# Edge counts of a two-layer GNN: windows of 6 destinations instead of 9, and a third of the window fetches issued by ScalarE

## The reference

```python
def _sage_sum(h, src, dst, Ws, Wn, b):
    h_neigh = jax.ops.segment_sum(h[src], dst, num_segments=N_NODES)
    return h @ Ws + h_neigh @ Wn + b
h = jnp.maximum(_layernorm(x, axis=-1), 0.0)
h = _sage_sum(h, src, dst, Ws1, Wn1, b1)
h = _sage_sum(h, src, dst, Ws2, Wn2, b2)
return x + h
```

## Time and profile before

| | us |
|---|---|
| median of 3 runs (lowest to highest) | 632.31 (631.12 to 633.39) |
| the profiled execution, own time | 634.33 |
| its span | 632.5 |
| TensorE busy | 618.4 (98%) |
| VectorE busy | 359.3 (57%) |
| GpSimd busy | 259.8 (41%) |
| ScalarE busy | 162.2 (26%) |

### The profile page before, as it was taken

One profiled execution on the slowest core, in us unless ns is written; L12 is line 12 of the kernel. 1 busy time (PEld: TensorE's weight loads), 2 busy tenths in 40 slices (PEclk: granted clock), 3 DMA queues, 4 the chain that ended last, 5 costly groups with the idle time before them and its releaser, 6 DMA issues.

```text
span 632.5 us, 8980 instructions
## 1 busy us (share of the span) xinstructions
PE 618.4 (98%) x3274; PEld 538.7 (85%) x3274; DVE 359.3 (57%) x543; ACT 162.2 (26%) x269; POOL 259.8 (41%) x234
## 2 busy tenths in 40 slices
PE   6999999999999999999999999999999999999996
PEld 5778777776999999999999987888888888888885
DVE  5764899761357456483412293135384867667563
ACT  5444443232011111101203111321234221222320
POOL 5232495111197586687820168204032204735000
PEclk9999999999999999999999999999999999999999
DMA  8711432232278967869761766444422235414153
GB/s 297 228 46 38 116 91 56 39 103 74 86 277 310 323 222 275 308 209 326 269 233 49 254 222 240 155 145 166 149 68 84 81 119 168 165 62 139 32 220 124
DMA packets 77128, 103.92 MB, mean 164 GB/s; under 512 B 25826, under 2 KB 44268, under 8 KB 77079
## 3 DMA queue, kind: packets, MB, share of 16 engines
q1 hardware_dynamic: 54550, 86.74, 41.0%
q10 hardware_dynamic: 22528, 16.53, 8.4%
HBM read 65.15 MB, written 38.10 MB: 163 GB/s over the span
## 4 chain that ended last, share of the span: by engine, by line
PE 94%; DVE 1%; POOL 1%; ACT 1%; DMA 1%; issue 1%; SPq 0%; ACTq 0%; POOLq 0%; DVEq 0%
PE PS L1368 30%; PE PS L1333 17%; PE PS L1205 15%; PE PS L1341 14%; PE PS L1405 13%; PE PS L1197 3%; PE PS L1231 1%; DMA xin<-x_in 1%; POOL W L615 0%; POOL norm L623 0%; ACT hbuf L777 0%; DVE HT L964 0%; ACT HT L768 0%; DVE stats L955 0%; DVE stats L956 0%
## 5 line engine op out<-in xcount | busy, mean ns | idle before, releaser
L1368 PE MATMUL PS<-right,left 128*128 128x512 f32 x840 | 190.9, 389 | 0.4 <-DVE left L1168 0.4
L1368 PEld LDWEIGHTS PS<-right,left 128*128 128x128 f32 x840 | 157.6, 188 | 33.4 <-DVE left L1168 0.8
L1205 PE MATMUL PS<-W,HT 128*128 128x512 f32 (+1 forms) x456 | 115.1, 399 | 1.1 <-ACT y_out L742 0.7
L1333 PE MATMUL PS<-HT,W_st 128*128 128x416 f32 (+1 forms) x576 | 110.2, 351 | 1.3 <-issue 1.3
L1333 PEld LDWEIGHTS PS<-HT,W_st 128*128 128x128 f32 x576 | 108.0, 188 | 2.4 <-issue 1.7
L705 POOL TENSOR_TENSOR left_sum<-h1T 128x640 f32<-128x640 f32 x24 | 43.4, 1811 | 159.0 <-PE PS L1368 119.4
L1205 PEld LDWEIGHTS PS<-W,HT 128*128 128x128 f32 (+1 forms) x456 | 81.3, 186 | 19.3 <-ACT y_out L742 1.5
L1341 PE MATMUL PS<-AT,y_st 128*128 128x416 f32 (+2 forms) x480 | 91.8, 351 | 0.0
L1341 PEld LDWEIGHTS PS<-AT,y_st 128*128 128x128 f32 (+1 forms) x480 | 89.9, 188 | 0.7
L672 POOL TENSOR_TENSOR prep_sum<-quarters 128x512 f32<-128x512 f32 x40 | 60.3, 1509 | 40.9 <-PE PS L1205 19.9
L677 POOL TENSOR_TENSOR prep<-prep_sum,prep 128x512 fp32r<-128x512 f32 x40 | 58.5, 1465 | 27.2 <-DVE prep L1098 27.2
(11 more groups left out here) (111 smaller groups left out, 550.2 us busy)
## 6 DMA issues: line engine op xcount, KB each, us to landing
sums_dram<-prep SPq DMA_DIRECT2D x40, 512.0 KB, 3.6
right<-sums_dram SPq DMA_DIRECT2D x40, 512.0 KB, 3.2
a_dram<-a_stage SPq DMA_DIRECT2D x20, 320.0 KB, 5.9
a_left<-a_dram SPq DMA_DIRECT2D x20, 320.0 KB, 3.7
y_dram<-y_out ACTq DMA_DIRECT2D x18, 256.0 KB, 2.3
y_st_raw<-y_dram ACTq DMA_DIRECT2D x8, 576.0 KB
s<-x_in SPq DMA_DIRECT2D x18, 256.0 KB
out<-s SPq DMA_DIRECT2D x18, 256.0 KB
```

The source lines that it names most:

```text
L1205: ins = nc.tensor.matmul(PS[:r, bank, :], HT[:, a, k, t * P:t * P + r], W[:, k, b, :], start=first and m == 0, stop=last and m == 2)
L1333: ins = nc.tensor.matmul(PS[:, banks[c], 0:w_], W_st[:, a, k, :], HT[:, b, k, o_:o_ + w_], start=k == 0 and m == 0, stop=False)
L1368: ins = nc.tensor.matmul(PS[:, BANKS2[g % 8], :], left[:, k, a, i * P:(i + 1) * P], right[:, KB - 1 - k, b, :], start=k == 0 and j == 0, s ...
```

## The change

Windows hold 6 destinations instead of 9 and rows 2 edges instead of 3, so there are 210 windows instead of 140, in 21 fetches instead of 14, 105 pairs instead of 70. A window takes two matmuls of 60 columns instead of three of 90; a group is 8 windows instead of 5 (27 groups instead of 28); the ring of one-hots holds 14 pairs instead of 8. Seven of the 21 fetches are issued by ScalarE, one window at a time, from its ordered queue: window n of fetch a at the event of window 10a - 56 + 3n, or at window 0 where that is negative. Two buffers of the prologue move into the room of the one-hots, and the general path is fitted to the new sizes (ANY, TRIO).

NW, NFETCH, NCOL, NG, NS, NSAMP and EROWS follow from the constants: 210, 21, 60, 27, 105, 33, 20,625 (before 140, 14, 90, 28, 70, 22, 13,750).

```diff
--- before.py
+++ after.py
@@ -21,12 +21,12 @@
 HI, LO = 0, 1
 PRODUCTS = ((HI, HI), (HI, LO), (LO, HI))
 CH = ((0, 416), (416, 416), (832, 418))
-WIN = 9
+WIN = 6
 NW = 2 * -(-N // (2 * WIN))
 FETCH = 10
 NFETCH = -(-NW // FETCH)
-ROW = 3
-ROWX = 12
+ROW = 2
+ROWX = 8
 EROWS = E // ROW
 SAMPLE = 5
 EP = 125
@@ -34,19 +34,22 @@
 RPP = EPP // ROW
 NSAMP = RPP // SAMPLE
 KEY = WIN + 2
-ANY = 12
+ANY = 17
 NCOL = NT * WIN
-GROUP = 5
+GROUP = 8
 NG = -(-NW // GROUP)
-HOT = 8
+HOT = 14
 NS = NW // 2
 SPF = FETCH // 2
+TRIO = 3
+ACT_FETCHES = (4, 7, 10, 13, 16, 18, 20)
+FETCH_AHEAD = 56
 SLAB_LAG = 8
 EPS = 1e-5
 EARLY = 8
 LEAD, SPAN = 0, 80
 LO_LAG = 10
-HOT_AHEAD = 6
+HOT_AHEAD = 8
 WARM, FILL = 20, 4
 
 KB = KF // 2
@@ -228,6 +231,11 @@
             yield ("y1", ends[p])
         if event[0] == "count" and last_of_group(event[1]):
             yield ("count", group_of(event[1]))
+        if event[0] == "count":
+            for a in ACT_FETCHES:
+                for n, w in enumerate(fetched(a)):
+                    if max(a * FETCH - FETCH_AHEAD + 3 * n, 0) == event[1]:
+                        yield ("fetch", w)
         if p in slabs:
             yield ("load", slabs.index(p))
         if event == ("y1", 2 * NT - 1, 6):
@@ -295,8 +303,9 @@
         ident = at("ident", [P, P], F32, o); o += up(P * 4)
         edge_f16 = at("edge_f16", [EP, RPP, ROWX], F16, o); o += up(RPP * ROWX * 2)
         edge_ints = at("edge_ints", [EP, 2, EPP], I32, o); o += up(2 * EPP * 4)
-        src_parts = at("src_parts", [EP, 2, EPP], I32, o)
-        samples = at("samples", [EP, NSAMP, NW], F16, o); o += up(max(NSAMP * NW * 2, 2 * EPP * 4))
+        src_parts = at("src_parts", [EP, 2, EPP], I32, R0)
+        samples = at("samples", [EP, NSAMP, NW], F16, R0)
+        assert max(NSAMP * NW * 2, 2 * EPP * 4) <= HOT_END - R0
         pad_row = at("pad_row", [P, ROWX], F16, o); o += up(ROWX * 2)
         assert o <= W0, o - W0
 
@@ -493,7 +502,8 @@
             sp.wait_ge(rows_saved, 32)
             sp.wait_ge(row_found, 1)
             for a in range(NFETCH):
-                load_windows(a)
+                if a not in ACT_FETCHES:
+                    load_windows(a)
 
 
             def quarter(what, row, col, k, to):
@@ -838,9 +848,24 @@
                     PS[:, COUNT_BANKS[g % 2], 0:n * NCOL].rearrange("p (w c d) -> p c w d", w=n, c=NT),
                     ACT.Copy, accum_out=degree[:, g:g + 1]).then_inc(counts_saved, 1)
 
+            rows_of_fetch = {}
+
+            def load_window(w):
+
+                a = w // FETCH
+                if a not in rows_of_fetch:
+                    _, rows_of_fetch[a] = nc.values_load_multi_w_load_instructions(
+                        row_i[0:1, fetched(a)[0]:fetched(a)[-1] + 1], engines=(mybir.EngineType.Activation,), min_val=0, max_val=EROWS,
+                        skip_runtime_bounds_check_because="a count of sampled edges times 5, less 5 and at least 0: at most EROWS - 5")
+                act.dma_start(window_edges[:, w, :], edge_rows[bass.ds(rows_of_fetch[a][w % FETCH], P), :]).then_inc(windows_in[a], 16)
+
+            act.wait_ge(rows_saved, 32)
+            act.wait_ge(row_found, 1)
             for what, n in scalar_order():
                 if what == "slab":
                     w_high(n)
+                elif what == "fetch":
+                    load_window(n)
                 elif what == "load":
                     load_w(n)
                 elif what == "w_st":
```

More of the change, by code:

```diff
@@ L1084, in _ @@
                     dve.wait_ge(g_self, NT + 3 * t + 3)
[L1085 to L1088, removed]
+                    with dve.Fori(0, RPP // TRIO) as trio:
+                        for q in range(TRIO * ROW):
+                            row, i = divmod(q, ROW)
+                            dve.wait_ge(g_free, trio * (TRIO * ROW) + (t * EPP + q + 1))
                             nc.vector.tensor_scalar(any_m[:EP, q % 2, :], iota_m[:EP, :, 0],
-                                                    edges[:, bass.ds(pair * 2 + odd, 1), 0, i], None, ALU.is_equal)
+                                                    edges[:, bass.ds(trio * TRIO + row, 1), 0, i], None, ALU.is_equal)
                             nc.vector.tensor_scalar(any_n[:EP, q % 2, :], any_iota[:EP, :, :].rearrange("p c d -> p (c d)"),
-                                                    any_key[:, bass.ds(pair * 2 + odd, 1), i], None, ALU.is_equal).then_inc(g_ready, 1)
+                                                    any_key[:, bass.ds(trio * TRIO + row, 1), i], None, ALU.is_equal).then_inc(g_ready, 1)
                 dve.wait_ge(g_written, 16 * NT)
@@ L1311, in _ @@
                         nc.tensor.matmul(PS[:, bank, 0:n * P], zeros[:EP, :], any_n[:EP, 0, c * P:(c + n) * P], start=True, stop=False)
-                    with pe.Fori(0, RPP // 2) as pair:
-                        for q in range(2 * ROW):
-                            pe.wait_ge(g_ready, pair * (2 * ROW) + (t * EPP + q + 1))
+                    with pe.Fori(0, RPP // TRIO) as trio:
+                        for q in range(TRIO * ROW):
+                            pe.wait_ge(g_ready, trio * (TRIO * ROW) + (t * EPP + q + 1))
                             for bank, (c, n) in enumerate(ACH):
```

## The result

| | before | changed |
|---|---|---|
| median, us (lowest to highest, 4 runs each) | 631.71 (630.70 to 633.39) | 641.82 (640.23 to 644.65) |
| ratio to before, 95% interval | | 1.0146 (1.0115 to 1.0178) |
| profiled execution, own time / span | 634.33 / 632.5 | 640.23 / 638.5 |
| end of the first stage in its profile | 156.42 | 164.91 |

The change costs 10.1 us by the medians, 9.2 (7.3 to 11.2) by the ratio. The two profiled executions lie 5.9 apart, since before's is slower than all its timed runs and the changed kernel's as fast as its fastest. Of the 8.5 us by which the first stage ends later in the trace, the untouched later stages hand back 2.5: the idle time ahead of the second stage is 0.41 us for 1.26, and its matmuls of 416 and 418 columns took 349 ns on average where they had taken 351.

The account below looks back on a forecast made before the run. TensorE, busy 98% of the span, was taken to bound the kernel. Terms 4.4 - 5.3 - 0.2 + 10.5 = +9.5 us (rounded) take the median from 632.31 to 641.8 (profiled 643.8); range 634 to 650.

Parts of the forecast that it names:

- The signs that it named: First stage and prologue: L1197 5 us less busy, samples 7.4 us, ScalarE ending TensorE's waits, stage 1 ending 9 us later.
- Counting matmuls: TensorE's blocks in the first stage: 420 matmuls of 60 columns at 30.6 ns instead of 43.1, -5.3 us.
- Sampling: Prologue: VectorE's comparison grows to 7.37 us, TensorE waits 2.6, its sampling matmuls take 3.05: +4.4 us.
- SyncE: Its fetch queue: still 14 fetches, ending at 138.2, window 190 countable from about 141, covered by TensorE's lateness.
- ScalarE: First stage: 70 window issues and 7 row loads in its ordered queue make TensorE wait for evictions, +10.5 us.
- The reason: First stage: ScalarE's issues and landing waits, standing before evictions in its queue, make TensorE wait, +10.5 us, the deciding term.
- narrow matmuls no shorter: Rival, counting blocks: matmuls stay at 43 ns, total +12.8 us, 645.1; chance 0.13.
- SyncE as the bound: Rival, first stage: ScalarE's waits vanish and SyncE's last windows decide, +2.5 us with the tail, 634.8; chance 0.06.
- Not slower: Rival, first stage: ScalarE's sequencer keeps ahead of TensorE, no new wait, 631.2, or 629.0 if half of sampling hides; chance 0.2.
- Row loads of 2.58 us each: Rival, ScalarE's queue: loads of ten row numbers cost 2.58 us instead of 1.68, +15.7 us, 648.0; chance 0.08.

Follow-up runs that it names:

- the experiment with fetches in the prologue: Changed kernel with ScalarE's fetches 4 and 7 (20 windows) issued in the prologue, order of loads, w_high and saves kept: 641.08 us, ratio to before 1.0135.
- the experiment on the clock: Changed kernel with 24 idle transposes where TensorE waits for the samples: 640.69 us, ratio to before 1.0121.
- the two combinations: Changed kernel, sampling by rows, 30 ScalarE windows issued in the prologue, w_high 12 events behind; the second spreads ScalarE's later fetches: 635.21 (1.0019) and 631.04 us (0.9953).
- the first experiment: Changed kernel with w_high 15 events behind its slab instead of 8 and w_low 17 instead of 10: 639.22 us, ratio to before 1.0082.

## Why the prediction was right, and where its terms were off

The forecast was +9.5 us, 641.8; measured were +10.1 (+9.2 by the ratio), 641.82. For a profiled execution it said 643.8, and that took 640.23, +5.9. The signs that it named came: ScalarE's L846 and L752 (L836 and L742 before) end TensorE's waits between 80 and 97 us, with 3.39 us in one piece ahead of tile 10. The terms were less exact than the sum, and that they met was partly luck:

- *Counting matmuls*, -5.3 forecast: 43.1 - 28.8 = 14.3 ns by 420 is -6.0, so a matmul at 60 columns has 3.8 ns beside its columns, not 5.6. The whole group:

```profile
L1222 PE MATMUL PS<-hot_n,hot_m 128*128 128x60 f16 x420 | 16.9, 193 | 3.1 <-ACT AT L846 2.8
...
L846 ACT ACTIVATE AT<-PS 128x480 fp32r<-128x480 f32 x26 | 14.8, 569 | 31.7 <-issue 16.5 <-PE PS L1222 14.8 <-ACT y_out L752 0.4
```

  It is 16.9 us busy for 23.1. The 81 ns of the Trainium skill ("TensorE: Matmul & The Clock Gate", Back-to-back issue gap), given for 128 columns, is far from both spacings of this trace; no weight load holds them above 28.8 ns at 60 columns.
- *Sampling*, +4.4: the wait (2.6) was right. The matmuls were mis-sized: 4.74 us for 3.05, because I took full clock behind an idle time. VectorE's three small instructions of find_rows were 0.5 us quicker. The first block comes 4.85 us later after allowing for the one slab more ahead of it, and as this trace was 0.56 us ahead at 26 us, sampling took 5.4 for the 4.4 forecast.
- *SyncE*: its last issue starts at 139.4, forecast 138.2; covered, as said, though narrowly (the 0.57 us for window 190 in the experiment with fetches in the prologue).
- *ScalarE*, +10.5: counted from start to start, the waits forecast as 2.2, 2.2, 0.8, 4.2 and 0.3, 1.0 and 0.5 were 2.2, 0.6, 0.3, 3.6 and none, 0.2 and 0.1, with 1.1 more, mostly ahead of the blocks at 114.6 and 117.7: about 8.0 for 11.2. What I left out is the clock: 1.3 us in the slabs and the block from 83.66 on, which only shortened the wait behind them (the experiment on the clock shows that wait at 1.44 for 0.43), and 1.6 in the slabs from 94.57 on. 8.0 and 2.9 less the 1.1 that before loses by the same count is 9.8. It is near the forecast because waits taken too long and a clock not thought of came out together, which is luck. The row loads aren't what was too large. Their median is under the 1.68 taken from SyncE, but the two ahead of tile 8's eviction took 1.22 and 2.19 us, as much as assumed (at 76.4 and 83.4 us; all seven in ns, min/median/max):

```profile
L857 ACTq TENSOR_LOAD <-row_i x7: 1006/1215/2452, 76.4 to 134.7; - x7
```

  The queue was at tile 8's bank at 94.5 for the 95.8 forecast; which of its steps I had too dear there isn't taken apart.

- *The reason* stood, but I gave one cause for what are two. The prediction put the waits on the issues and on the order of the landings together. The runs show that either is enough for 3 to 4 us at tile 8's bank: order alone (3.37 with ScalarE issuing no window; 2.41 and 1.53 in the kernel before), issues alone (3.55 and 1.61). They don't add up, since each can hide inside the other: with the early issues taken away the wait was 3.52, where it had been 3.39 with them.
- *Rivals*: narrow matmuls no shorter, and SyncE as the bound, are excluded by the rows above. "Not slower" is what the two combinations reach by design. Row loads of 2.58 us each didn't come (1.2 in the median).

Terms of the trace together: 5.4 - 6.0 - 0.2 + 9.8 = +9.0, less the 0.6 by which this trace was ahead at 26 us: 8.4, against 8.5 read at the stage's end and the 9.2 (7.3 to 11.2) of the ratio.

## What to carry to other kernels

A lag that is counted in entries of a mixed order changes its meaning when the entries change size: check every such constant against time when a tile is made smaller. Sum up each ordered queue, issues and landing waits included, and not only the engines' busy time: ScalarE was 25% busy and still set the pace. Where TensorE is made to wait two microseconds or more, price what follows it at the clock that its trace shows, above all behind the last such wait. And check the releaser that a row names against the time at which it had ended: the 1.45 us that were put down to hot_n were ScalarE's.

## What I had not expected of the hardware

The granted clock in three short stretches: TensorE idle for 2.6 us, then 0.66 granted over the next 5 us (33 matmuls of 210 columns at 144 ns, 94 with the clock kept); idle for 3.4 us, then 0.60 over 4. Where the first experiment left idle times of 1.4 to 1.6 us, the slabs after the two at 81.8 and 86.1 went at full speed. But the last idle time alone doesn't tell: in the kernel before with the order changed, the three matmuls behind 2.41 us of idle time took 0.96 us, and the three behind the next one, of 1.53 us, took 1.65 (0.50 granted from 88 to 92 us). Keeping TensorE at work with 24 idle transposes kept the clock at 1.00. What exactly the chip goes by was not tried.
